# Turns of the probabilities and reads of the memory placed between products of the feed-forward, on one core

## What is computed

```python
# per segment; 8 heads, DK = DV = 64, L = 128
sq = elu(q_s) + 1.0
att_mem = sq @ mem / (sq @ z)                       # read of the memory
sk = elu(k_s) + 1.0
mem = mem + einsum('bhlk,bhlv->bhkv', sk, v_s)      # its update
z = z + sk.sum(axis=-2, keepdims=True).transpose(0, 1, 3, 2)
att_dot = softmax(einsum('bhik,bhjk->bhij', q_s, k_s) * scale)
att = gate * att_mem + (1.0 - gate) * (att_dot @ v_s)
x = layernorm(x + att @ Wo)
h = relu(x @ Wq1.T + b1)                            # 512 -> 2048
x = layernorm(x + h @ Wq2.T + b2)                   # 2048 -> 512
```

## Time and profile before

| | |
|---|---|
| median of 3 runs | 1904.53 us (1903.65 to 1907.4) |
| span of the profiled execution | 1901.0 us |
| TensorE matmuls busy | 98% of the span |
| VectorE busy | 77% |
| ScalarE busy | 53% |
| GpSimd busy | 42% |
| mean granted TensorE clock | 0.990 |
| one group in the steady part | 56.76 us |

### The profile page before, as it was taken

One profiled execution on the slowest core, in us unless ns is written; L12 is line 12 of the kernel. 1 busy time (PEld: TensorE's weight loads), 2 busy tenths in 40 slices (PEclk: granted clock), 3 DMA queues, 4 the chain that ended last, 5 costly groups with the idle time before them and its releaser, 6 DMA issues.

```text
span 1901.0 us, 44707 instructions
## 1 busy us (share of the span) xinstructions
PE 1853.6 (98%) x16575; PEld 1311.9 (69%) x16575; DVE 1461.3 (77%) x2969; ACT 1003.4 (53%) x2426; POOL 794.9 (42%) x790
## 2 busy tenths in 40 slices
PE   5689999999999999999999999999999999999998
PEld 3566677766677766677766677766677766677765
DVE  7867777787777787877787877787877777777774
ACT  5765555555554555554545555545555545555541
POOL 1713344444344444345444345444335444344443
PEclk9889999999999999999999999999999999999999
DMA  8412333222333223233323333322333323323110
GB/s 271 124 22 48 57 63 66 52 49 59 63 59 65 55 47 61 59 61 64 64 39 61 62 59 62 65 39 60 60 60 63 69 36 60 61 58 63 36 23 23
DMA packets 556422, 117.49 MB, mean 62 GB/s; under 512 B 529824, under 2 KB 533808, under 8 KB 555696
## 3 DMA queue, kind: packets, MB, share of 16 engines
q1 hardware_dynamic: 556208, 114.64, 29.4%
HBM read 50.54 MB, written 16.80 MB: 35 GB/s over the span
## 4 chain that ended last, share of the span: by engine, by line
PE 94%; ACT 2%; DVE 2%; issue 1%; POOL 1%; DMA 0%; POOLq 0%; ACTq 0%; DVEq 0%
PE bank L444 12%; PE bank L430 12%; PE bank L431 12%; PE bank L445 12%; PE bank L280 6%; PE bank L281 6%; PE bank L282 6%; PE bank L368 3%; PE bank L294 3%; PE bank L412 3%; PE bank L413 3%; PE bank L411 3%; PE bank L347 3%; PE bank L296 3%; PE bank L295 3%; PE bank L399 2%
## 5 line engine op out<-in xcount | busy, mean ns | idle before, releaser
L430 PE MATMUL bank<-yt,w1t 128*128 128x256 f16 x2048 | 453.9, 273 | 0.0
L431 PE MATMUL bank<-yt,w1t 128*128 128x256 f16 x2048 | 453.9, 273 | 0.0
L1141 ACT ACTIVATE prob<-bank,exp_bias,gscalars 128x128 f32<-128x128 f32 x512 | 227.4, 455 | 358.6 <-DVE exp_bias L723 350.2
L444 PE MATMUL bank<-w2t,arena 128*128 128x512 f16 x1024 | 388.4, 379 | 0.0
L445 PE MATMUL bank<-w2t,arena 128*128 128x512 f16 x1024 | 388.1, 379 | 0.0
L1187 ACT ACTIVATE arena<-bank,b_scaled,wscalars 128x256 f32<-128x256 f32 x512 | 262.4, 568 | 207.1 <-PE bank L431 154.5
L858 DVE CAST arena<-arena 128x512 f16<-128x512 f32 x256 | 155.3, 607 | 92.8 <-ACT arena L1187 92.1
L1317 POOL TENSOR_TENSOR att_mem<-att_mem,gate_in 128x512 f32<-128x512 f32 x60 | 87.9, 1466 | 330.3 <-DVE att_mem L762 330.3
L430 PEld LDWEIGHTS bank<-yt,w1t 128*128 128x128 f16 x2048 | 200.4, 98 | 23.2 <-issue 0.3
L431 PEld LDWEIGHTS bank<-yt,w1t 128*128 128x128 f16 x2048 | 200.3, 98 | 22.8
L1395 POOL TENSOR_TENSOR arena<-arena 128x512 f16<-128x512 f32 x128 | 155.1, 1212 | 87.2 <-DVE arena L858 87.2
(11 more groups left out here) (191 smaller groups left out, 4384.6 us busy)
## 6 DMA issues: line engine op xcount, KB each, us to landing
rows<-in_L_attn_x SPq DMA_DIRECT2D x32, 512.0 KB, 3.7
out_rows<-rows SPq DMA_DIRECT2D x64, 256.0 KB, 2.3
x_blocks<-in_L_attn_x SPq DMA_DIRECT2D x248, 64.0 KB, 2.8
sk<-sk_t SPq DMA_DIRECT2D x480, 32.0 KB, 2.0
att_dot<-att_mem SPq DMA_DIRECT2D x480, 32.0 KB, 2.0
y_blocks<-rows SPq DMA_DIRECT2D x480, 32.0 KB
arena<-in_L_ffn_W SPq DMA_DIRECT2D x6, 1024.0 KB, 5.3
w2t<-in_L_ffn_W SPq DMA_DIRECT2D x2, 1024.0 KB, 13.4
```

The source lines that it names most:

```text
L430: pe.matmul(ps[:, c], w1t[:, k, cols], yt[:, g % 2, :, k], start=k == 0, stop=False)
L431: ins = pe.matmul(ps[:, c], w1t[:, k, cols], yt[:, g % 2, :, KT + k], start=False, stop=k == KT - 1)
L444: pe.matmul(banks[own][:], h_hi[:, f, toks], w2t[:, f, :], start=f == 0, stop=False)
L1141: ins = act.activation(prob[:, t, at], ps[:, c], ACT.Exp, scale=gcol(g, G_EXP), bias=exp_bias[:, t, at:at + 1], accum_out=row_sum[:, t, h: ...
```

## The change

Three things are edited. First, the turns of the probabilities no longer stand in blocks of four: each of the four follows two products of a piece of `ffn_down` (`down_and_turn_p`). The three halves (0, 1), (1, 0) and (1, 1), which stood together ahead of piece 2 of sequence 1, now stand in its pieces 0, 1 and 2. Half (0, 0) stands in piece 1 of sequence 0. Second, the memory gets zero-padded blocks: for a pair of heads `mem` is 128 rows by 2 x 65 columns, in which head 2c fills rows 0 to 63 of the first 65 columns and head 2c + 1 rows 64 to 127 of the others. A read is then four fp32 products of 128 rows and 130 columns, in place of eight of 64 rows and 65 columns, and each follows two products of a piece (`down_and_read`): the read (g, 0) stands in piece 3 of sequence 0, the read (g, 1) in piece 3 of sequence 1, which moves behind `attend(g, 0)`. Third, `take` gets `ahead`, by which the halves (1, 0) and (1, 1) swap their banks. DVE's list keeps its order; `mem_add` and `reset_memory` become two instructions each, of 64 partitions. `y_blocks` moves into a free part of `arena`.

```diff
-        mem = sb("mem", [P, LIVE * TG, NPAIR, DV1])
+        mem = sb("mem", [P, LIVE * TG, NPAIR, 2, DV1])
...
+        AHEAD = {(1, 0): 1, (1, 1): -1}
...
-            def take(job):
+            def take(job, ahead=0):
-                b = 2 + turn[0] % 4
+                b = 2 + (turn[0] + ahead) % 4
...
+            def down_and_turn_p(g_down, t_down, piece, g, t, half):
+                turns = 0 <= g < NG
+                first = piece * FT // PIECES
+                fs = range(first, first + FT // PIECES) if 0 <= g_down < NG else ()
...
+                for i in range(4):
+                    if fs:
+                        f = first + i
+                        pe.matmul(down[:], h_hi[:, f, toks], w2t[:, f, :], start=f == 0, stop=False)
+                        last = pe.matmul(down[:], h_lo[:, f, toks], w2t[:, f, :], start=False, stop=f == FT - 1)
+                    if turns:
+                        if i == 0:
+                            b = take(("p", g, t, half), AHEAD.get((t, half), 0))
+                            ps = banks[b][:].rearrange("p (h t) -> p h t", h=4)
+                            pe.wait_ge(sem["pexp"], by_half(g, t, half))
+                        ins = pe.transpose(ps[:, i], prob[:, t, 4 * half + i], ident32[:])
...
+            def down_and_read(g_down, t_down, piece, g, t):
...
+                for c in range(NPAIR):
+                    if fs:
+                        f = first + c
+                        pe.matmul(down[:], h_hi[:, f, toks], w2t[:, f, :], start=f == 0, stop=False)
+                        last = pe.matmul(down[:], h_lo[:, f, toks], w2t[:, f, :], start=False, stop=f == FT - 1)
+                    if reads:
+                        _, seg, live = place(g)
+                        if c % 2 == 0:
+                            b = take(("read", g, t, c // 2))
+                            ps = banks[b][:, 0:4 * DV1].rearrange("p (c n) -> p c n", c=2)
+                            bank_free[b] = (sem["attm"], by_half(g - LIVE, t, c // 2))
...
+                        ins = pe.matmul(ps[:, c % 2], sq_t[:, t, c], mem[:, live * TG + t, c].rearrange("p e n -> p (e n)"),
                                         start=True, stop=True)
...
-                turn_p(g, 0, 0)
-                ffn_down(g - 2, 0, 1)
+                down_and_turn_p(g - 2, 0, 1, g, 0, 0)
...
                 scores(g, 1)
-                read_memory(g, 0)
-                ffn_down(g - 2, 0, 3)
-                ffn_down(g - 2, 1, 0)
+                down_and_read(g - 2, 0, 3, g, 0)
...
-                ffn_down(g - 2, 1, 1)
-                turn_p(g, 0, 1)
-                turn_p(g, 1, 0)
+                down_and_turn_p(g - 2, 1, 0, g, 0, 1)
+                down_and_turn_p(g - 2, 1, 1, g, 1, 0)
                 turn_y(g - 1, 0)
-                turn_p(g, 1, 1)
-                ffn_down(g - 2, 1, 2)
...
+                down_and_turn_p(g - 2, 1, 2, g, 1, 1)
                 turn_y(g - 1, 1)
-                ffn_down(g - 2, 1, 3)
...
                 attend(g, 0)
-                read_memory(g, 1)
+                down_and_read(g - 2, 1, 3, g, 1)
...
-                dve.tensor_tensor(m, banks[bank_of["upd", g, t]][:, 0:NPAIR * DV1].rearrange("p (c n) -> p c n", c=NPAIR), m,
-                                  ALU.add).then_inc(sem["mem"], 1)
+                ps = banks[bank_of["upd", g, t]][:, 0:NPAIR * DV1].rearrange("p (c n) -> p c n", c=NPAIR)
+                for e, own in enumerate((slice(0, DK), slice(DK, P))):
+                    ins = dve.tensor_tensor(m[own, :, e], ps[own], m[own, :, e], ALU.add)
+                ins.then_inc(sem["mem"], 1)
```

More of the change, by code:

```diff
@@ L351, in read_memory @@
[L351 to L365, removed]
-                for c in range(NPAIR):
-                    for e, own in enumerate((slice(0, DK), slice(DK, P))):
-                        ins = pe.matmul(ps[e][:, c], sq_t[own, t, c], mem[own, live * TG + t, c],
+            def down_and_turn_p(g_down, t_down, piece, g, t, half):
+                turns = 0 <= g < NG
+                first = piece * FT // PIECES
+                fs = range(first, first + FT // PIECES) if 0 <= g_down < NG else ()
+                toks = slice(t_down * P, (t_down + 1) * P)
+                down = banks[6 + t_down]
+                if fs:
+                    wait_down(g_down, t_down, piece)
+                for i in range(4):
+                    if fs:
[8 more added lines that the diff above has]
+                        ins = pe.transpose(ps[:, i], prob[:, t, 4 * half + i], ident32[:])
+                if fs and piece == PIECES - 1:
+                    last.then_inc(sem["ffn2"], 1)
+                if turns:
+                    ins.then_inc(sem["pturn"], 1)
+                    bank_free[b] = (sem["pt"], by_half(g, t, half))
@@ new lines, in down_and_read @@
+            def down_and_read(g_down, t_down, piece, g, t):
+                reads = LIVE <= g < NG
+                first = piece * FT // PIECES
+                fs = range(first, first + FT // PIECES) if 0 <= g_down < NG else ()
+                toks = slice(t_down * P, (t_down + 1) * P)
+                down = banks[6 + t_down]
+                if fs:
+                    wait_down(g_down, t_down, piece)
+                for c in range(NPAIR):
+                    if fs:
+                        f = first + c
[7 more added lines that the diff above has]
+                            bank_free[b] = (sem["attm"], by_half(g - LIVE, t, c // 2))
+                        if c == 0:
+                            pe.wait_ge(sem["elu"], 4 * g + 4)
+                            if seg:
+                                pe.wait_ge(sem["mem"], by_t(g - LIVE, t))
+                            else:
+                                pe.wait_ge(sem["reset"], by_t(g // (LIVE * NSEG) * LIVE + live, t))
+                        ins = pe.matmul(ps[:, c % 2], sq_t[:, t, c], mem[:, live * TG + t, c].rearrange("p e n -> p (e n)"),
@@ L369, in read_memory @@
                                         start=True, stop=True)
-                ins.then_inc(sem["num"], 1)
+                if fs and piece == PIECES - 1:
+                    last.then_inc(sem["ffn2"], 1)
+                if reads:
+                    ins.then_inc(sem["num"], 1)
             def attend(g, t):
@@ L432, in ffn_up, with wait_down @@
                 ins.then_inc(sem["ffn1"], 1)
+            def wait_down(g, t, piece):
+                if piece == 0 and g:
+                    pe.wait_ge(sem["res1"], by_t(g - 1, t))
+                pe.wait_ge(sem["h_dve"], 4 * g + piece + 1)
+                pe.wait_ge(sem["h_pool"], 4 * g + piece + 1)
             def ffn_down(g, t, piece):
@@ L750, in read_scale @@
                     return
[L751 to L755 removed]
+                for j in range(2):
+                    ps = banks[bank_of["read", g, t, j]][:, 0:4 * DV1].rearrange("p (h n) -> p h n", h=4)
+                    hs = slice(4 * j, 4 * j + 4)
+                    if j == 0:
                         dve.wait_ge(sem["sc2"], g + 1)
@@ L1576, in move_y @@
                     sp.wait_ge(sem["yt"], by_t(g - 1, 1))
-                move_blocks(y_blocks[:], rows[:, g % NX], sem["yblocks"])
+                move_blocks(y_blocks, rows[:, g % NX], sem["yblocks"])
             def put_out(g, t):
```

33 lines of the change are left out of this document (9 added, 24 removed).

## The result

| | before | changed |
|---|---|---|
| median of 4 runs each | 1904.97 us (1903.65 to 1907.4) | 1919.16 us (1917.2 to 1919.4) |
| span of the profiled execution | 1901.0 us | 1917.3 us |
| a group without a late transfer | 56.77 us | 56.94 us |
| last scores of group 2 start at | 173.54 us | 179.78 us |
| TensorE's share of the chain that ended last | 94% | 90% |

The ratio is 1.0067, 95% interval [1.0054, 1.0079]: slower, as forecast, but by 14.2 us and not by 5.7. 1919 lies above the range, which ended at 1917.

A forecast was written before the change was run, and what follows sets the result against it. TensorE was taken to bound the kernel, without standing still from group 2 on. Gates of 0.45 less 0.26 from the reads gave +0.19 a group, times 30 +5.7 us: median 1904.5 to 1910.2 us, range 1896 to 1917.

The forecast's parts named there:

- Turns, 0: TensorE's turns of the probabilities: spread between products, each still takes 0.109 us, so the term is 0.
- The rival of the load: Turns are paced by their weight load and take 0.055 us when spread: -0.23 a group, 1897.6 us; chance 0.05.
- Reads, -0.26 a group: The padded reads on TensorE at 0.11 us an instruction: -0.01 for read (g, 0), -0.25 for read (g, 1).
- The rival of the double price: A padded read instruction costs 0.22 us: +53 us on top, 1963 us; chance 0.05.
- The two gates: TensorE's new waits at halves (0, 1) and (1, 1): 0.45 us a group in all; chance 0.52.
- T11: First turn of half (1, 1): at 7.97 us behind the last scores, in place of 7.52 without any wait.
- T01: First turn of half (0, 1): at 3.48 us behind the last scores, where TensorE arrives at 3.20, a wait of 0.28.
- the second gate: Half (1, 1) waits for its probabilities, late since DVE keeps `read_scale(g, 0)` ahead of the maxima: 0.45 us in all.
- Over 30 groups: The steady group's +0.19 us was multiplied by 30 groups (2 to 31), giving +5.7 us.
- Covered, by 0.1 us alone: Third product of read (g, 1): bank free at 12.05, TensorE there at 12.14; waiting rival up to +0.4 a group, chance 0.08.
- The first gate: Half (0, 1) waits 0.28 us for ACT to free the bank of the scores (1, 0).
- Costed at nothing: Split `mem_add` on DVE (some 0.8 us a group, covered), moved `y_blocks` and doubled fills: no cost to TensorE.

The follow-up runs named there:

- q_turn_later: n_repaired with half (0, 1) turned one piece later and half (1, 0) in one block behind it: 1897.08 us, ratio 0.9969 to the kernel before.
- l_read_behind: Kernel before with padded reads directly behind a 512-column product, turns in old blocks, c_dve_order's DVE order, `attend` banks exchanged, `read_scale(g, 1)` ahead of `att_scale(g, 0)`: 1899.87 us.
- f_padded_in_place: Kernel before with the padded memory alone, each read as eight instructions at its old place: 1902.85 us, ratio 0.9989.
- c_dve_order: Changed kernel with the maxima of the scores (1, 1) ahead of `read_scale(g, 0)` on DVE: 1913.24 us, ratio 1.0043 to the kernel before.
- a_start_banks: Changed kernel with the exchange of banks only from group 2 on: 1914.63 us, ratio 1.0053 to the kernel before.
- k_late_bank: Changed kernel with the second bank of the read (g, 1) and the bank of `attend(g, 1)` exchanged: 1914.66 us, ratio 1.0059 to the kernel before.
- i_no_swap: Changed kernel without the exchange of banks between halves (1, 0) and (1, 1): 2001.16 us in one run.
- m_behind_old_dve: l_read_behind with `read_scale(g, 0)` ahead of the maxima on DVE again: 1934.61 us in one run.
- n_repaired: Changed kernel with the repairs of a_start_banks, b_start_all, c_dve_order and k_late_bank together: 1902.6 us, ratio 0.9998 to the kernel before.
- b_start_all: a_start_banks with half (1, 1) also ahead of the weight turns of group 0: 1911.7 us, ratio 1.0043 to the kernel before.

## Why the prediction was right and wrong

- **Turns, 0.** Right: 0.11 between products as in the block. `q_turn_later` and `l_read_behind` have the same group of 56.51 with spread and with blocked turns. The rival of the load falls.
- **Reads, -0.26 a group.** Right for the change, where each stands behind 512 columns. The instruction is 0.11, the lower bound. The rival of the double price falls as it was put, but something of it is real: the first load of a read costs 0.1 where nothing long stands ahead (`f_padded_in_place`, `l_read_behind`).
- **The two gates.** Right in place, cause and nearly in size. T11, by which the sum goes, came at 7.94 (7.97 forecast), and the sum is +0.17 for +0.19. T01 was mis-sized: it was to wait 0.28 and takes 0.36 in place of 0.22, so it waits 0.14. From ACT's end to the turn pass 0.05 there (3.31 to 3.36), where 0.18 were taken, 0.15 of them from the first group; at T11 they are 0.15 (7.79 to 7.94). `c_dve_order` removes the second gate, `q_turn_later` both.
- **"Over 30 groups", all alike.** This is the step that failed. The sum took 5.7 us from the group of the steady part, times 30, and nothing from elsewhere; elsewhere were 11.3 of the 16.2 us. The turns of groups 0 and 1 had been read, with their waits, but the change was not followed through them: the exchange of banks meets TensorE's `turn_y` in group 1, and the weight turns stand ahead of the half (1, 1) in group 0. Together 6.2 us in this trace. The 4.0 of the bank is shown by its waits, by their absence in `a_start_banks`, and by the distance from group 1 to group 2 in thirteen traces; what the weight turns cost can't be told from the scatter of the start.
- **"Covered, by 0.1 us alone".** The third product of the read (g, 1) is forecast at 12.14 and stands there. The room ahead of it is 0.30 (11.84 to 12.14) and not 0.1. The text even names what would break it, a late `y_blocks`, and gave it 0.08 and up to 0.4 a group. It breaks in groups 3, 7 and 10 for late transfers, in 15 and 16 for the longer `reset_memory`, and in 6 for a late start of DVE, 5.0 us in all. The trace of before had late transfers; they were invisible as time, since nothing behind them was tight. `k_late_bank` shows the mechanism, in groups 6 and 15. The first gate has no slack at all, and there group 29 loses 0.3 more.
- **Costed at nothing.** For `mem_add` it held: two instructions of 64 partitions take 426 ns each, so DVE has the 0.4 more for each addition, and the group of `q_turn_later` has no wait. For the doubled fills it didn't: "no list that TensorE waits for" overlooked that `reset_memory` stands ahead of the last `pt_lo`, 0.3 in each of two groups.

In sum: +4.9 from the group, +6.2 from the start, +5.3 from the seven groups, less some 0.3 that the kernel before loses to its own, are 16.1; 16.2 were measured at the last scores of group 31. What makes the issues of `y_blocks` slow on SyncE, and the engines late in groups 6 and 29, stays open; no run was made for it.

## What to carry to other kernels

A gain that is read from the steady group holds only if the change is followed through the first groups as well, where other jobs take part in the same rotation of banks. Where a cover is a few tenths of a us (0.30 here), look in the trace of before for events that scatter by more than that, even if they cost nothing yet, and price each of them. And give a result its room: turning one half one piece later was worth 0.20 in each group here (56.71 to 56.51), some 6 us, where spreading the turns gave nothing.

## What was not expected of the hardware

- The first fp32 load ahead of a group of products costs 0.1 us if no product of 512 columns stands ahead, and nothing if one does (1.00 and 0.98 in `f_padded_in_place` against 0.90 and 0.89 in `l_read_behind`).
- A wait of 2.11 us on TensorE is followed by 3.4 us at 1.2 GHz in sixteen of 28 groups of `i_no_swap`, with 1.7 us on top of the wait; a single wait of 2.00 in group 7 of `a_start_banks` is followed by such a stretch too, and that group loses 3.9. The wait of 1.60 in group 7 of the change is followed by none, nor is that of 1.02 in any group of `m_behind_old_dve`.
- Ahead of group 2 the same lists come out 3.5 and 3.9 us apart in two pairs of kernels (`n_repaired` and `b_start_all`, `f_padded_in_place` and `l_read_behind`), with granted clocks of 0.87 and 0.84 from 60 to 130 us in both.
